# One routed feed-forward kernel: sums of squares for its scales, one z operation, the last scaling on VectorE, and scatters ahead of younger roots on GpSimd

## The reference

```python
diffs = x[:, 1:] - x[:, :-1]                    # 8 last differences form a window
normed = diffs / mag                            # mag = norm of a difference
g = softmax(2 * normed @ guide.T / g_norm)      # 64 guidance vectors
blended = 0.6 * normed + 0.4 * g @ guide
traj = sum(blended * pos_w * tanh(2 * mag)) / sum(pos_w * tanh(2 * mag))
x = layernorm(x + traj)
probs = softmax(x @ Wr + br);  e = argmax(probs);  gate = max(probs)     # 8 experts
xn = (x - mu) * rsqrt(var + eps) * ln_g + ln_b
y = relu(xn @ W1[e] + b1[e]) @ W2[e] + b2[e]    # 128 -> 512 -> 128
x = layernorm(x + y * gate)
```

## Time and profile before

| | us |
|---|---|
| median of three runs (lowest, highest) | 218.2 (217.67, 218.41) |
| the profiled execution | 218.13 |
| its span | 216.3 |
| mean granted TensorE clock | 0.811 |

### The profile page before, as it was taken

The page is one execution under the profiler, slowest core; times in us unless marked ns, Lnnn a source line. Parts: engine busy times, 40 slices in busy tenths (PEclk is TensorE's granted clock), DMA queues, the critical chain, the costliest instruction groups (busy, mean ns, idle before and its releaser), DMA issues.

```text
span 216.3 us, 5485 instructions
## 1 busy us (share of the span) xinstructions
PE 150.0 (69%) x1395; PEld 125.7 (58%) x1395; DVE 171.1 (79%) x792; ACT 141.6 (65%) x425; POOL 122.3 (57%) x210
## 2 busy tenths in 40 slices
PE   0057974998777898674510069999899999899600
PEld 0015753685756487573400059899798898788400
DVE  2447789878998988986868517999999999999910
ACT  2357627483835567737712078999999999998530
POOL 4322213423728775877877240377777787678670
PEclk9999997575888597855555558999999999999955
DMA  5996770000100100001015140222222222220000
GB/s 147 355 364 193 213 200 0 3 0 2 39 13 22 34 25 25 27 28 50 25 52 150 36 89 16 50 66 60 70 74 77 71 64 70 75 64 23 31 10 2
DMA packets 16417, 15.76 MB, mean 73 GB/s; under 512 B 2810, under 2 KB 13142, under 8 KB 16386
## 3 DMA queue, kind: packets, MB, share of 16 engines
q1 hardware_dynamic: 13458, 10.83, 18.3%
q0 software_dynamic: 2272, 4.27, 6.0%
q10 hardware_dynamic: 656, 0.30, 0.5%
HBM read 10.52 MB, written 5.33 MB: 73 GB/s over the span
## 4 chain that ended last, share of the span: by engine, by line
PE 21%; ACT 20%; POOL 18%; DVE 15%; issue 13%; DMA 5%; DVEq 2%; SPq 1%; ACTq 1%; POOLq 1%
POOL rows L357 12%; ACT OUT L672 4%; PE bank L433 3%; PE bank L540 3%; DMA XN<-in_attn_embeddings 3%; ACT xs L649 3%; DVE hl L986 3%; ACT xt L654 3%; PE bank L454 3%; POOL rstd L345 2%; POOL R L349 2%; ACT sq L559 2%; ACT hh L663 2%; PE bank L526 2%; PE bank L528 2%
## 5 line engine op out<-in xcount | busy, mean ns | idle before, releaser
L388 POOL DMA_INDIRECT out<-OUT,tok x39 | 40.4, 1037 | 25.1 <-issue 23.9
L357 POOL DMA_INDIRECT rows<-R,place x32 | 34.0, 1061 | 9.0 <-issue 9.0
L526 PE MATMUL bank<-sel,bias 96*128 96x128 bf16 x156 | 35.2, 226 | 0.0
L540 PE MATMUL bank<-W2hl,hh 128*128 x156 | 32.6, 274 | 3.5 <-issue 2.6
L528 PE MATMUL bank<-xh,W1h 128*128 128x128 f16 x156 | 34.9, 224 | 0.0
L530 PE MATMUL bank<-xh,W1l 128*128 128x128 f16 x156 | 34.7, 223 | 0.0
L529 PE MATMUL bank<-xl,W1h 128*128 128x128 f16 x156 | 34.7, 222 | 0.0
L433 PEld LDWEIGHTS bank<-V,C 128*128 128x128 f32 x128 | 24.9, 299 | 11.2 <-issue 11.2
L986 DVE SCALAR_TENSOR_TENSOR hl<-bank,hh 128x512 f16<-128x512 f32 x39 | 26.9, 690 | 3.0 <-ACT hh L663 2.8
L433 PE MATMUL bank<-V,C 128*128 128x129 f32 x128 | 26.8, 393 | 3.0 <-DVE Y L753 3.0
L543 PE MATMUL bank<-W2hl,hl 128*128 x156 | 27.9, 219 | 0.0
(11 more groups left out here) (161 smaller groups left out, 448.9 us busy)
## 6 DMA issues: line engine op xcount, KB each, us to landing
XR<-rows SPq DMA_DIRECT2D x39, 66.0 KB, 2.0
W<-in_ffn_W SPq DMA_DIRECT2D x1, 2048.0 KB, 11.3
X<-in_attn_embeddings SPq DMA_DIRECT2D x2, 512.0 KB, 9.0
X<-in_attn_embeddings SPq DMA_DIRECT2D x1, 768.0 KB
out<-OUT,tok POOLq DMA_INDIRECT x39
XN<-in_attn_embeddings SPq DMA_DIRECT2D x2, 256.0 KB, 8.2
rows<-R,place POOLq DMA_INDIRECT x32, 2.4
C<-in_constants SPq DMA_DIRECT2D x1, 428.0 KB, 5.2
```

The source lines that it names most:

```text
L357: pool.indirect_dma_start(out=rows[:, :], out_offset=bass.IndirectOffsetOnAxis(ap=place[u % 4][:, k:k + 1], axis=0), in_=R[u % 4][:, k, :] ...
L388: pool.indirect_dma_start(out=out[:, :], out_offset=bass.IndirectOffsetOnAxis(ap=tok[k][:, 0:1], axis=0), in_=OUT[k][:, :], in_offset=None ...
L526: pe.matmul(h, bias3[:, c * P:(c + 1) * P], sel, start=True, stop=False)
L540: pe.matmul(y[:, 0:2 * D], hh[k][:, c * P:(c + 1) * P], w, start=c == 0, stop=False)
```

## The change

The scales come from sums of squares, which ACT takes in i = 0 to 3 with an accumulating Square, one matmul with ones sums over partitions (in PE's step 3), POOL takes four roots (`weight_roots`) and DVE computes the powers of two in window 4. The high halves are made in i = 5 to 8. The gate is multiplied with the last scale in the first half already (`gated`), so the row holds it, and the scatter of unit 0 waits for it. POOL issues two scatters of unit i-4 before the roots of unit i-2 and the two others after them. In the blocks, both halves of y go to the same 128 columns and one z operation adds them to the row; the last scaling moves from ACT to DVE; stores take the token numbers from the row itself, of which there are now sixteen buffers.

```diff
-        W1h = sb("W1h", [P, E, FF], F16)              # and W1l; W2hl = [P, E, FC, 2 * D]
+        W1h = [sb(f"W1h{c}", [P, E, P], F16) for c in range(FC)]   # and W1l, W2h, W2l
-        XR = [sb(f"XR{i}", [P, ROW]) for i in range(UN)]
+        XR = [sb(f"XR{i}", [P, ROW]) for i in range(RN)]           # RN = 16
+        HI_AT = (5, 6, 7, 8)
 ...  # SP: the six bias loads and both gb loads now follow W1, W2 follows x2 (all were last)
-            def load(count, k):
-                after(sp, every["z0"], blocks(count(-1), k))
-                after(sp, every["token"], blocks(count(-1), k))
+            def load(b):
+                if b >= RN:
+                    sp.wait_ge(stored[b % UN], 16 * ((b - RN) // UN + 1))
 ...  # POOL
+            def weight_roots():
+                pool.wait_ge(s["roots_in"], 1)
+                pool.tensor_tensor(roots[:, 0:4], norms[:, 0:4], half[:, :], ALU.pow).then_inc(s["roots"], 1)
-            def scatter(u):
+            def scatter(u, tiles=range(NT)):
                 pool.wait_ge(s["placed"], u + 1)
+                pool.wait_ge(s["gated"], u + 1)
-            for i in range(-1, NU + 4):
+            for i in range(-1, NU + 2):
+                if 5 <= i:
+                    scatter(i - 5, range(2, NT))
                 if i + 1 < NU:
                     mag_roots(i + 1)
-                if 2 <= i <= NU + 1:
+                if i == 4:
+                    weight_roots()
+                if 4 <= i:
+                    scatter(i - 4, range(2))
+                if 2 <= i:
                     std_roots(i - 2)
-                if i >= 4:
-                    scatter(i - 4)
-            def token(count, k):
 ...  # cg = gate * scl and tok = row number, two POOL operations per block, go
+            scatter(NU - 3, range(2, NT))
+            scatter(NU - 2)
+            scatter(NU - 1)
             def store(count, k):
-                pool.wait_ge(every["token"], blocks(count(0), k))
-                pool.wait_ge(every["out"], blocks(count(0), k))
+                pool.wait_ge(every["out"], b + 1)
+                pool.wait_ge(row_loaded[b % RN], 16 * (b // RN + 1))
-                    ... IndirectOffsetOnAxis(ap=tok[k][:, 0:1], axis=0)
+                    ... IndirectOffsetOnAxis(ap=XR[b % RN][:, D + 2:D + 3].bitcast(I32), axis=0)
-            steps([(-3, store), (3, token)])
+            steps([(0, store)])
 ...  # PE: transpose of mx and matmul with mx4 at i == 5 go
+                if i == 3:
+                    pe.wait_ge(s["sums"], 6)
+                    pe.wait_ge(s["gains"], 1)
+                    pe.wait_ge(s["shifted"], 1)
+                    pe.matmul(sums_ps, ones[:, :], sums[:, :], start=True, stop=True).then_inc(s["sums_ps"], 1)
+                pe.matmul(y[:, 0:D], sel16[...], bias3[:, FF:FF + D], start=True, stop=False)
                 for c in range(FC):
-                    pe.matmul(y[:, 0:2 * D], hh[k][:, c * P:(c + 1) * P], w, start=c == 0, stop=False)
-                    m = pe.matmul(y[:, 0:D], hl[k][:, c * P:(c + 1) * P], wh, start=False, stop=c == FC - 1)
+                    pe.matmul(y[:, 0:D], hh[k][:, c * P:(c + 1) * P], wh, start=False, stop=False)
+                    pe.matmul(y[:, 0:D], hl[k][:, c * P:(c + 1) * P], wh, start=False, stop=False)
+                    m = pe.matmul(y[:, 0:D], hh[k][:, c * P:(c + 1) * P], wl, start=False, stop=c == FC - 1)
 ...  # ACT, between nT_(i) and et(i)
+            def squares_w1(q):
+                if q == 0:
+                    act.wait_ge(ld["w1"], 16)
+                act.activation(junk[:, :], W1[:, 2 * q:2 * q + 2, :], ACT.Square, accum_out=sums[:, 8 + q:9 + q])
+                act.drain()
-                if i >= NU - 1:
-                    weights_hi(i - NU + 1)
+                if 0 <= i < 2:
+                    squares_w1(2 * i)
+                    squares_w1(2 * i + 1)
+                if i == 2:
+                    squares_bias()
+                if 2 <= i < 4:
+                    squares_w2(2 * i - 4)
+                    squares_w2(2 * i - 3)
+                if i in HI_AT:
+                    weights_hi(HI_AT.index(i))
-                if i == 7:      # bias3; the bias_m piece moves from 8 to 6
+                if i == 5:
-            steps([(5, b_xs), (1, b_hh), (-3, b_fin), (4, b_xt), (-2, b_sd), (4, b_xh)])
+            steps([(5, b_xs), (1, b_hh), (4, b_xt), (-2, b_sd), (4, b_xh)])
 ...  # DVE: maxima1, maxima2, mx4 go; scales(step) stands in window 4, not 6, and ends so:
+                if i == 4:
+                    scales(6)
+                    for step in range(7, 11):
+                        dve.drain()
+                        scales(step)
+                    dve.drain()
+                    gated(0)
+            def gated(g):
+                if g >= 4:
+                    dve.wait_ge(scattered[g % 4], 16 * NT * (g // 4))
+                ts(R[g % 4][:, :, D], gate[:, :], scl[:, 3:4], None, ALU.mult).then_inc(s["gated"], 1)
-                if 8 <= i <= 9:
-                    split_bias(i - 8)
+                if 6 <= i <= 7:
+                    split_bias(i - 6)
-                stt(z0[k][:, :], bank[5 + k % 2][:, 0:D], cg[k][:, :], XR[k][:, 0:D], ALU.mult, ALU.add)
-                stt(z[k][:, :], bank[5 + k % 2][:, D:2 * D], cg[k][:, :], z0[k][:, :], ALU.mult, ALU.add)
+                stt(z[k][:, :], bank[5 + k % 2][:, 0:D], XR[x][:, D:D + 1], XR[x][:, 0:D], ALU.mult, ALU.add)
-            def b_shift(count, k):
+            def b_fin(count, k):
+                after(dve, stored[k], count(0) * 16)
+                dve.wait_ge(every["rec"], blocks(count(0), k))
+                ts(OUT[k][:, :], z[k][:, :], mv2[k][:, 0:1], sd[k][:, 1:2], ALU.subtract, ALU.mult)
-            steps([(1, b_hl), (-1, b_mv), (0, b_z0), (-2, b_rec), (0, b_z), (-2, b_shift), (0, b_bn), (4, b_xl)])
+            steps([(1, b_hl), (-1, b_mv), (0, b_z), (-2, b_rec), (0, b_bn), (-2, b_fin), (4, b_xl)])
```

More of the change, by code:

```diff
@@ L115, in build @@
         bias3 = sb("bias3", [96, FF + D], BF16)
-        mx = sb("mx", [P, 16])
-        mx4 = sb("mx4", [4, 8])
+        sums = sb("sums", [P, 16])
+        junk = sb("junk", [P, 2 * FF], BF16)
+        norms = sb("norms", [P, 8])
+        roots = sb("roots", [P, 12])
+        gate = sb("gate", [P, NT])
         scl = sb("scl", [P, 16])
@@ L180, in build @@
         mv2 = [sb(f"mv2{i}", [P, 2]) for i in range(UN)]
-        sd = [sb(f"sd{i}", [P, 3]) for i in range(UN)]
+        sd = [sb(f"sd{i}", [P, 2]) for i in range(UN)]
         OUT = [sb(f"OUT{i}", [P, D]) for i in range(UN)]
-        ld = {n: sem("ld_" + n) for n in ("cst", "guide", "small", "x0", "x1", "x2", "x3", "w1", "w2", "bias")}
+        ld = {n: sem("ld_" + n) for n in ("cst", "guide", "small", "x0", "x1", "x2", "x3", "w1", "w2", "bias", "gb")}
         names = ("zeroed diff sumsq guarded rmag var_in rstd var2_in r2 mags tanh scales n np nT_ps nT_sb sims_ps ET "
                  "infl_ps V traj_ps y x1c x1 xT_ps xT_sb logits_ps shifted exped onehot rank_ps placed "
-                 "counted guide_sq guide_norm guided guideT_ps guideT split_hi split_lo maxima maxT_ps max4 maxb_ps max_read scales_w "
+                 "counted guide_sq guide_norm guided guideT_ps guideT split_hi split_lo sums sums_ps sums_read gains roots_in roots gated scales_w "
                  "bias_hi bias_rest tot_ps pad_rows table pads_ready").split()
@@ L193, in build @@
         padded = sem("padded")
-        names2 = "xs xh xl hl z".split()
+        names2 = "xs xh xl hl".split()
         t = {n: [sem(f"b_{n}{i}") for i in range(UN)] for n in names2}
-        every = {n: sem("every_" + n) for n in "token xT_ps xt h_ps hh y_ps z0 bn mv sd rec shift out".split()}
+        every = {n: sem("every_" + n) for n in "xT_ps xt h_ps hh y_ps z bn mv sd rec out".split()}
         seen = sem("seen")
-        row_loaded = [sem(f"row_loaded{i}") for i in range(UN)]
+        row_loaded = [sem(f"row_loaded{i}") for i in range(RN)]
         stored = [sem(f"stored{i}") for i in range(UN)]
@@ L308, in _ @@
                     load_rows(b + UN // 2)
-                load(lambda d, turn=b // UN: turn + d, b % UN)
+                load(b)
             for k in range(UN):
@@ L467, in _ @@
             for i in range(0, NU + 3):
-                if i == 5:
-                    pe.wait_ge(s["maxima"], 1)
-                    pe.wait_ge(s["xT_sb"], 3)
-                    pe.transpose(xT_ps[0:4, 0:P], mx[:, 0:4], ident).then_inc(s["maxT_ps"], 1)
                 if i < NU:
@@ L478, in _ @@
                     sims(i)
-                if i == 5:
-                    pe.wait_ge(s["max4"], 1)
-                    pe.matmul(xT_ps[:, P:P + 4], ones[0:4, :], mx4[:, 0:4], start=True, stop=True).then_inc(s["maxb_ps"], 1)
                 if 1 <= i <= NU:
@@ L660, in b_hh @@
             def b_hh(count, k):
-                act.wait_ge(every["token"], blocks(count(0), k))
                 act.wait_ge(every["h_ps"], blocks(count(0), k))
@@ L665, in b_sd @@
```

(6 more changed lines are left out.)

225 lines of the change are left out of this document (101 added, 124 removed).

## The result

The changed kernel takes 229.73 us (median of four runs, 229.22 to 231.78) where the kernel before takes 218.31 beside it: 1.053 times as long [1.044, 1.062]. It was to be 215.5. The profiled execution has a span of 227.7 against 216.3, so 11.4 us are to be found.

The account below looks back on a forecast made before the run. It took POOL's scatters to bound the first half and PE, DVE and ACT, all full, the blocks. From the profiled 218.13: 218.13 - 0.1 + 0.2 - 1.5 - 1.2 = 215.5 us, range 211.8 to 218.9.

Parts of the forecast that it names:

- Part 2: The blocks: PE becomes the bound at a beat (transpose to transpose) of 1.77, 34 beats 63.4 against 65.0; term -1.5.
- the sum for DVE: Blocks: DVE's pitches per block total 1.73 with the last scaling at 0.20, or 1.88 at 0.35, nothing won.
- DVE stays the bound: Rival, blocks: the scaling costs DVE 0.30 or more, the beat is 1.84, total 216.9 us; chance 0.14.
- The rule on shared interfaces: Blocks: GpSimd contends with DVE for SBUF; stores taking 2.00 would make POOL the bound at 2.3; not in the sum.
- Part 1, the squares: First half, start: two ACT squares between nT and ET delay ET(0) by 1.15, from 16.15 to 17.3.
- V(2) is where it was: First half: the start of V, DVE's beat per unit, unchanged for unit 2; V(3) only 0.2 later, at 47.8.
- Part 1, the new wait: Window 4: scatter(0) waits for gated(0) at 55.9, roots queue behind; DVE waits 2.5 for rstd(2), V(4) at 62.35.
- Part 1, windows 5 to 8: First half: 28.8 from V(4) to V(7), less 1.4, plus 1.6, plus 0.4; V(7) at 91.7, 2.3 later.
- POOL's packing: First half, after V(7): the new order wins back 2.6 us of POOL's idle time; last scatter ends at 120.4.
- The splits: Start of the blocks: the lo splits after the last places end at 125.1 instead of 122.0; term +0.2.
- Part 3: The tail: faster last blocks -0.5, y(38) -0.15, its end to the last store's issue 4.4 (-0.55); term -1.2.
- The slower rival: First half: roots behind scatter(0) behind gated(0), PE at 1.2 GHz; splits 4.5 late, total 219.9 us; chance 0.17.

Follow-up runs that it names:

- b1: The changed kernel with each block's expert a constant, so no register instructions stand ahead of PE's products (output of other experts): 218.97 us, 1.001.
- b2: The kernel before with hh times W2 as two products of 128 columns instead of one of 256, in three of four chunks: 224.03 us, 1.027.
- f3: The changed kernel without ACT's two squares of step 0 (half of W1 left out of the sums): 227.89 us, 1.045.
- f2: The changed kernel with POOL's old order in every step, both roots and then four scatters: 227.24 us, 1.042.
- i3: The changed kernel with 256 columns of y again (low half not added) and POOL's old order in every step: 217.82 us, 0.995.
- h1: The kernel before with each block's expert a constant, so no register instruction stands ahead of a product (output of other experts): 216.99 us, 0.994.
- f1: The changed kernel with the roots of unit 2 ahead of the two scatters in POOL's step 4 alone: 226.51 us, 1.040.
- j1: The very kernel of g2 again in another session: 216.17 us, 0.990.
- g2: The changed kernel with 256 columns of y (low half not added), unit 2's roots ahead of step 4's scatters and no squares in step 0: 225.66 us, 1.033.
- b3: The changed kernel with y again as four products of 256 columns and four of 128, the low half not added: 220.87 us, 1.011.
- g3: b3 with eight products per block taking weights from another buffer, so 20 register instructions per block instead of 12: 248.10 us, 1.139.

## Why the prediction was wrong

- **Part 2, "PE: ... becomes twelve times 128 ... 0.72 becomes 0.735. Beat 1.77"** is the step that failed most. The columns were counted rightly (b1: 1.75) and the instructions between them not at all. The split adds four products and four register instructions to a queue that hid twelve; b2 shows it alone costing 5.5 us of blocks. Term -1.5, measured +5.05. The pauses grew too: they were 2.35 to 2.83 and are 2.76 to 3.29. b1 keeps the line that loads the numbers, and the pauses are gone; no profile shows whether its program still loads them, so what in reading and using the numbers makes the pause stays open.
- The other lines of Part 2 held. DVE's scaling has a pitch of 0.24, between the 0.20 taken and the 0.35 above it; without the split the beats are 1.745 and 34 take 62.3, better than the 63.4 forecast. (The rows that the sum for DVE names give 1.75 and 1.90, where it says 1.73 and 1.88; nothing hung on it.) "DVE stays the bound" did not happen; in b1, at 1.75, PE and DVE are both without a gap (12.00 of 12), so the edits leave DVE no more room than they leave PE. Stores take 0.98, not 2.00: a scatter beside a split is again 2.00 (at 93.13). The rule on shared interfaces (the Trainium skill, GPSIMD Engine Reference, Key points) agrees with that scatter, and no store of the blocks shows it. From 166 to 177 the stores overlap DVE's operation with two SBUF inputs, xl, by 0.09 at most, so that they hardly test the rule.
- **Part 1, the squares.** ET(0) came at 17.77 for 17.3, close: W1 had landed at 15.3, not 14.6. But "V(2) is where it was" was wrong. V(3) was 49.36, not 47.8, and f3, with V(3) at 47.42, shows that the start's delay of about 2 is carried to the end. PE's clock, on which the prediction hung V(3), is not what made it late: from 30 to 45 the granted clock was 0.79, for 0.69 before. No run shows slack in this loop that takes up a late start.
- **Part 1, the new wait.** Its place was right and its size was not: 3.54 for 2.5. That V(3) was late moves both ends of the wait (gated(0) at 57.23 for 55.9). What lengthens it is the way from the gate product to the root's end, 4.7 for 3.8: the first scatter starts 0.92 behind the product's end, where 0.18 was taken. V(4) was 64.40 for 62.35.
- **Part 1, windows 5 to 8** failed by the most within the half: V(4) to V(7) took 32.2, not 29.35. DVE's waits behind POOL's scatters (0.50 and 0.76 before V(7)) had no term. But f2 and i3, both with the old order and no such waits, took 30.95 and 32.77, and kernels with the first half of before (before, b2, h1) took 28.81, 29.93 and 30.92. So the lateness is about 1 to 3 us, the executions differ by nearly as much, and its causes were not taken apart.
- POOL's packing worked as described: V(7) to the last scatter's end 29.3 for 31.1. The last issue waits for nothing but DVE. The landing, 3.48 for 2.34, had no term; it was 2.3 to 3.1 in the other runs that show it, so a part of it may not be the change's doing. The splits ended at 130.4, not 125.1, still ahead of the first transpose. Of the 6.4, f1 and f3 account for most; with both undone (j1, g2) the blocks still began 1.1 and 2.3 later than before, which stays open.
- **Part 3.** The end of y(38) to the last store is 4.47, forecast 4.4. But the three last blocks have PE's slow products too, 8.67 to the end of y(38) from the last transpose, 8.36 before: -0.16 in all for -1.2. That 4.4 came out is luck. In b3, whose PE keeps the forecast's pace, the last blocks take 7.73, as forecast, and the leg to the last store 4.82; b1 has 4.98. The last stores, 1.28 apart, queue up when PE is fast. The tail (last transpose to last store) is then 12.55, for 12.1 forecast: -0.75. b3's last matmul and last store:

```profile
206.06 0.22 PE L551 MATMUL bank<-W2hl,hl 128*128 x1
...
211.10 0.98 POOL L399 DMA_INDIRECT out<-OUT,XR  x1 [0.30 <-issue]
```

- The slower rival named the right mechanism in the first half (the root behind the scatter behind the gate product) and priced it at +4.5 with the splits; f1 gives 3.2 for it. None of the rivals had PE's queue. With the split undone (and the low half not added) the time is 220.9, and 216.2 with the two other parts undone too, near the forecast: its arithmetic described a kernel that was not there.

## What to carry to other kernels

Splitting a product into two of half the columns was free here only while PE's instructions arrived in time: count the register instructions ahead of products whose address is built at run time, let neighbouring products share an address, and measure the beat with constant addresses to see what they cost. PE's busy share didn't show this here; the starts did, compared with a clean stretch, and so did the busy time of the weight loads. Where a wait is added to an in-order queue, put what another engine's loop needs ahead of it: one swapped line gave back 3.2 us.

## What the runs showed of the hardware

- In g3 two of three products behind a register instruction start 0.11 us behind the one before, others 0.055 to 0.06 (b1, b3). Twelve in a block of 26 products are hidden (b3), 15 with 29 and 16 with 30 cost 0.2 a block (b2, the changed kernel), 20 with 26 cost 0.65 (g3).
- The pauses of every eight blocks, 0.5 to 1.0 us each in b3, vanish when the expert numbers are not used, though the line that loads them stays (b1; in h1 too, but for one beat of 2.24).
- GpSimd scales 128x128 in 0.80 us (0.97 until its next instruction), VectorE in a pitch of 0.24.
- One program carried stops of about 1 us every four blocks in one session (four runs, 225.4 to 227.6 us) and none in another (ten runs, 216.0 to 219.2). A surprising sum of parts is worth a second session before it is worth a theory.
